# A transformer block on one core: four part buffers, weights loaded between the stores, merged score loads

## What is computed

```python
# x: (2, 2048, 256); 16 query heads, 4 key/value heads, head width 16
h = layernorm(x)
q, k, v = h @ Wq + bq, h @ Wk + bk, h @ Wv + bv
scores = einsum('bghnd,bhsd->bghns', q, k)           # g: 4 query heads share a key head
attn = softmax(scores / 4, axis=-1)
x = x + einsum('bghns,bhsd->bghnd', attn, v) @ Wo + bo
x = x + ffn(layernorm(x))                            # three cycles of a coupling net (cn_*, gc_*)
x = x + attn_b(layernorm(x))                         # Wg1 @ Wg2 makes its sigmoid gate
x = x + ffn(layernorm(x))
```

## Time and profile before

| | |
|---|---|
| median of 3 runs | 2151.23 us |
| the profiled execution, its own time | 2154.36 us |
| its span | 2152.4 us |
| TensorE's mean granted clock | 0.961 of full |
| busy: PE, PEld, DVE, ACT, POOL | 93%, 38%, 84%, 70%, 7% |

### The profile page before, as it was taken

How to read it: one execution, slowest core, us unless ns; L and a number is a source line. 1 busy time by engine, 2 the same in 40 slices (tenths; PEclk the granted TensorE clock), 3 DMA queues, 4 the chain that set the end, 5 groups by cost and what they waited for, 6 DMA issues and landing times.

```text
span 2152.4 us, 47834 instructions
## 1 busy us (share of the span) xinstructions
PE 2008.2 (93%) x13990; PEld 821.5 (38%) x13990; DVE 1814.5 (84%) x3396; ACT 1496.7 (70%) x2955; POOL 159.8 (7%) x290
## 2 busy tenths in 40 slices
PE   6699999999999999999999999989985899998984
PEld 4323333333333333333333333344432566665431
DVE  6789999999999999999999999934557677776456
ACT  4438888888888888888888888844558544446656
POOL 1340000000000000000000000010004101002001
PEclk9769999999999999999999999999997999999996
DMA  6421121121122122122122122131000000000002
GB/s 165 136 67 43 44 72 52 44 71 53 43 71 53 43 71 54 42 71 55 42 69 56 42 70 56 34 126 46 1 1 1 1 0 1 1 0 1 1 1 79
DMA packets 110229, 101.30 MB, mean 47 GB/s; under 512 B 52240, under 2 KB 91424, under 8 KB 110096
## 3 DMA queue, kind: packets, MB, share of 16 engines
q1 hardware_dynamic: 110096, 99.92, 17.2%
HBM read 78.79 MB, written 20.77 MB: 46 GB/s over the span
## 4 chain that ended last, share of the span: by engine, by line
PE 82%; DVE 6%; ACT 4%; issue 3%; SPq 3%; DMA 1%; ACTq 0%; POOL 0%; DVEq 0%; POOLq 0%
PE ps L697 22%; PE ps L672 15%; PE ps L720 10%; PE ps L726 10%; PE ps L840 6%; PE ps L847 3%; PE ps L900 3%; PE ps L909 2%; PE ps L929 2%; PE ps L948 2%; ACT YT L1088 1%; PE ps L686 1%; PE ps L979 1%; SPq L423 1%; DVE mx L1395 1%
## 5 line engine op out<-in xcount | busy, mean ns | idle before, releaser
L1395 DVE TENSOR_REDUCE mx<-ps 128x1 f32<-128x512 f32 x2048 | 1279.7, 683 | 20.2 <-PE ps L672 15.4
L1088 ACT ACTIVATE YT<-ps 128x512 f32<-128x512 f32 x2048 | 1058.1, 606 | 253.4 <-PE ps L726 253.3
L697 PE MATMUL ps<-YT,work 128*32 128x512 f32 x4096 | 546.1, 605 | 0.0
L672 PE MATMUL ps<-work 64*128 64x512 bf16 x2048 | 460.8, 389 | 17.7 <-DVE mx L1395 14.2
L720 PE MATMUL ps<-work 64*128 64x512 bf16 x2048 | 401.7, 378 | 1.7
L726 PE MATMUL ps<-work 34*128 34x512 bf16 x2048 | 398.3, 378 | 0.0
L672 PEld LDWEIGHTS ps<-work 64*128 64x128 bf16 x2048 | 144.6, 93 | 622.0 <-DVE mx L1395 548.3
L720 PEld LDWEIGHTS ps<-work 64*128 64x128 bf16 x2048 | 162.1, 94 | 106.0 <-ACT YT L1088 31.7
L847 PE MATMUL ps<-work,c_s 128*128 128x512 f32 x192 | 101.5, 655 | 30.9 <-ACT work L1139 30.9
L697 PEld LDWEIGHTS ps<-YT,work 128*32 128x32 f32 x4096 | 80.7, 108 | 122.8 <-issue 86.9
L726 PEld LDWEIGHTS ps<-work 34*128 34x128 bf16 x2048 | 101.0, 94 | 49.0 <-issue 1.3
(11 more groups left out here) (176 smaller groups left out, 1781.2 us busy)
## 6 DMA issues: line engine op xcount, KB each, us to landing
work<-k_scr SPq DMA_DIRECT2D x640, 64.0 KB, 2.1
work<-q_scr SPq DMA_DIRECT2D x640, 32.0 KB, 1.8
o_scr<-o_sb SPq DMA_DIRECT2D x32, 256.0 KB, 2.2
X<-in_L_attn_a_x_dram SPq DMA_DIRECT2D x8, 512.0 KB, 7.4
work<-negt SPq DMA_DIRECT2D x256, 1.0 KB
work<-o_scr SPq DMA_DIRECT2D x16, 256.0 KB
work<-inv_scr SPq DMA_DIRECT2D x16, 256.0 KB
out_dram<-X SPq DMA_DIRECT2D x8, 512.0 KB, 2.9
```

Source lines behind the costliest of these rows:

```text
L672: mm(ps[:, bank_of[x], :], qa[rows, p, jp, qt * P:(qt + 1) * P], ka[rows, p, kc_ * CH:(kc_ + 1) * CH], start=True, stop=True).then_inc(a_m ...
L697: m = mm(ps[32 * j:32 * j + 32, 7, :], vst[:, p, t, :], prob(GROUP * t + j), start=t == 0, stop=t == KTILES - 1)
L1088: fn(prob(u), ps[:, S_BANK + u % S_RING, :], ACT.Exp, scale=HD ** -0.5).then_inc(exp_ok, 1)
L1395: dve.tensor_reduce(mx[:, p, at_:at_ + 1], ps[:, bank_of[x], :], AX_X, ALU.max).then_inc(a_max, 1)
```

## The change

- **Part buffers:** both batches take all four in turn, chunk c the buffer c mod 4. Waits for a free buffer are for the chunk four before. `part_a` now holds chunks 4 and 5 too, so SP's first score loads and GpSimd's fills of kc and vst wait for the stores of chunks 2 to 5.
- **Weights:** six of the 36 later weights after the stores of each of the chunks 0 to 5.
- **Score loads:** `load_queries` issues 4 DMAs in place of 8 (32 rows by 2 pieces of 1 KB) and `load_keys` 4 in place of 8; the source of a key load is the same 16 rows read twice, with the repetition as its outermost dimension (stride 0, count 2), and 32 partitions as its destination. Both first score loads stand after chunk 5, the first query loads after chunk 1.
- **Negated maxima of step 0:** ahead of the last part's store of chunk 7 instead of after all stores.
- **Gate:** `gate_turn` and `gate_product` stand among the 16 maxima ahead, at x = 2 and x = 8. ScalarE's wait for the last stores goes.
- **Constants:** VectorE's ten operations stand after its last maxima.

```diff
-LOADED_MAX = 16 * 16
-LOADED = 16 * (16 + 8)
+LOADED_MAX = 16 * 8
+LOADED = 16 * (8 + 8)
...
         def part(c, pt):
-            return (part_a if c < CPG else part_b)[:, c % 2, pt]
+            return (part_a, part_b)[c // 2 % 2][:, c % 2, pt]
...
         def buffer_of(c):
-            return c // CPG * 2 + c % 2
+            return c % CPG
...
             if c >= 0:
-                eng.wait_ge(p_st[pt][buffer_of(c)], STORED * (c % CPG // 2 + 1))
-                eng.wait_ge(k_st[pt][buffer_of(c)], 16 * (c % CPG // 2 + 1))
+                eng.wait_ge(p_st[pt][buffer_of(c)], STORED * (c // CPG + 1))
+                eng.wait_ge(k_st[pt][buffer_of(c)], 16 * (c // CPG + 1))
...
-            for dst, src in weights:
-                sp.dma_start(dst, src).then_inc(w_ld, 16)
+            def load_weights(part):
+                for dst, src in weights[part::FREE]:
+                    sp.dma_start(dst, src).then_inc(w_ld, 16)
...
                         row = g * HALF + r * FINE
-                        for jp in range(JP):
-                            sp.dma_start(q_dst[row:row + FINE, p, jp],
-                                         q_scr[s, 2 * jp + g, 0:2].rearrange("r d n -> (r d) n")).then_inc(done[p], 16)
+                        sp.dma_start(q_dst[row:row + FINE, p],
+                                     q_scr[s, g:GROUP:2, 0:2].rearrange("j r d n -> (r d) j n")).then_inc(done[p], 16)
...
                         row = g * HALF + r * FINE
-                        for part_row in (row, row + HD):
-                            sp.dma_start(k_dst[part_row:part_row + HD, p], k_scr[kv_of(s), r]).then_inc(done[p], 16)
+                        src = k_scr[kv_of(s), r].rearrange("(a d) n -> a d n", a=1).broadcast_to((2, HD, SEQ))
+                        sp.dma_start(k_dst[row:row + FINE, p], src).then_inc(done[p], 16)
...
                 if c == CPG - 1:
                     for pt in range(2):
-                        for p in range(2):
-                            sp.wait_ge(k_st[pt][p], 16 * CPG // 2)
+                        for c4 in range(CPG):
+                            sp.wait_ge(k_st[pt][c4], 16)
                     load_keys(ka, 0, 0, qa_ld)
+                if c == NCH - 1:
+                    sp.wait_ge(nm_t, 1)
+                    load_negated(0)
                 store(c, 2, p_low)
-                if c == 0:
+                if c < FREE:
+                    load_weights(c)
+                if c == 1:
                     stored(sp, 0, 0)
                     stored(sp, 1, 0)
                     for s in (0, 1):
                         load_queries(qa, s, s, qa_ld)
                 if c == CPG:
                     load_keys(ka, 1, 1, qa_ld)
-                    stored(sp, 2, CPG - 2)
-                    stored(sp, 2, CPG - 1)
-                    load_scores(0, 0)
-                if c == NCH - 2:
-                    load_scores(1, 1)
+                if c == CPG + 1:
+                    for pt in range(3):
+                        for c4 in range(2, CPG + 2):
+                            stored(sp, pt, c4)
+                    for s in (0, 1):
+                        load_scores(s, s)
...
-            sp.wait_ge(nm_t, 1)
-            load_negated(0)
             refill_max(0, 0)
...
             for x in range(AHEAD):
+                if x == 2:
+                    pe.wait_ge(w_ld, 16 * len(weights))
+                    gate_turn()
+                if x == 8:
+                    gate_product()
                 max_mm(0, 1, x)
-            pe.wait_ge(w_ld, 16 * len(weights))
-            gate_turn()
-            gate_product()
...
                     if c not in (CPG, CPG + 1):
                         wait(act, p_low, c - 1)
-                        stored(act, 0, c - 2)
+                    stored(act, 0, c - CPG)
...
-                if c not in (CPG, CPG + 1):
-                    stored(act, 1, c - 2)
+                stored(act, 1, c - CPG)
...
-            for pt in range(3):
-                for c in (NCH - 2, NCH - 1):
-                    stored(act, pt, c)
...
-                if c not in (CPG, CPG + 1):
-                    stored(dve, 2, c - 2)
+                stored(dve, 2, c - CPG)
...
             negated_turn(STEPS - 1)
+            constants()
...
-                stored(pool, 2, c - 2)
+                stored(pool, 2, c - CPG)
...
             for pt in range(3):
-                for c in (CPG - 2, CPG - 1):
+                for c in range(2, CPG + 2):
                     stored(pool, pt, c)
-            pool.wait_ge(p_low, CPG)
+            pool.wait_ge(p_low, CPG + 2)
             pool.memset(kc[FINE:FINE_M], 1.0).then_inc(kb_ones, 1)
```

More of the change, by code:

```diff
@@ L1354, in _, with constants @@
                 low(c)
[L1356 to L1361, removed]
-            dve.tensor_copy(e3_s[:], last_c[0:64, 1:2].broadcast_to((64, P))).then_inc(cols, 2)
-            dve.tensor_scalar(half_b[:, 0:1], bias[:, D4:D4 + 1], 0.5, None, ALU.mult)
-            dve.tensor_scalar(half_b[:, 1:2], bias[:, F3:F3 + 1], 0.5, None, ALU.mult).then_inc(c_dve, 1)
-            dve.memset(coup[:, 2:3], 0.1)
-            dve.tensor_scalar(coup[:, 1:2], bias[:, AR:AR + 1], 0.3, None, ALU.mult)
-            dve.tensor_scalar(coup[:, 3:4], bias[:, AR:AR + 1], 0.7, None, ALU.mult).then_inc(c_dve, 1)
+            def constants():
+                dve.wait_ge(w_ld, 16 * len(weights))
+                dve.tensor_scalar(ct_s[:, 0, :], c1_s[:, 1, :], bias[:, SG:SG + 1], -1.0, ALU.mult, ALU.mult).then_inc(c_tw, 1)
+                dve.tensor_scalar(ct_s[:, 1, :], c1_s[:, 0, :], bias[:, SG:SG + 1], None, ALU.mult).then_inc(c_tw, 1)
+                dve.tensor_copy(w4_s[0:64, 0:1], last_c[0:64, 0:1])
+                dve.tensor_copy(w4_s[64:P, 1:2], last_c[64:P, 0:1])
+                dve.tensor_copy(c4_s[:], last_c[:, 0:1].broadcast_to((P, P))).then_inc(cols, 1)
+                dve.tensor_copy(e3_s[:], last_c[0:64, 1:2].broadcast_to((64, P))).then_inc(cols, 2)
+                dve.tensor_scalar(half_b[:, 0:1], bias[:, D4:D4 + 1], 0.5, None, ALU.mult)
+                dve.tensor_scalar(half_b[:, 1:2], bias[:, F3:F3 + 1], 0.5, None, ALU.mult).then_inc(c_dve, 1)
+                dve.memset(coup[:, 2:3], 0.1)
+                dve.tensor_scalar(coup[:, 1:2], bias[:, AR:AR + 1], 0.3, None, ALU.mult)
+                dve.tensor_scalar(coup[:, 3:4], bias[:, AR:AR + 1], 0.7, None, ALU.mult).then_inc(c_dve, 1)
             def row_maxima(s, p):
```

## The result

The changed kernel takes 2161.21 us (median of 5 runs, 2159.77 to 2162.49) against 2151.23 us (5 runs, 2150.05 to 2154.16): 1.0041 times as long, 95% interval 1.0028 to 1.0053, so slower by about 0.4%. The prediction was 2161 us. That the number is right is luck: its account is wrong in two of its terms, and their errors happen to cancel. In what follows one execution of one kernel, k_split_scores (2503.47 us at a granted clock of 0.739, the others 0.960 to 0.963), is left out of its ratio as slow.

What follows compares the result with a forecast made beforehand. It took the lead-in before the first L726 as what could move, with TensorE-bound steps unchanged. Merged keys on two engines outweighed a 23.5 us gain: 2151.23 + 9.9 = 2161 us, range 2126 to 2176.

Steps and rivals of the forecast that it cites:

- Buffers: Lead-in: two ScalarE stops of about 6.3 us go, low(5) ends at 67.5 instead of 79.8, gaining 12.3 us.
- Constants: VectorE's ten operations at the end: about 2.1 us, at most 3.0, under 4.7 us of cover, so no cost.
- Gate: Lead-in, among the sixteen maxima: no stall counted, at most the 2 us of the small matmuls.
- The merged key load: Key loads: two DMA engines instead of sixteen, 14.3 us a load_keys, with all queued behind the keys waiting.
- rival A: Key loads spread over all engines or onto others than the stores: 23.5 or 20 us less; chance 0.20.
- the ledger of engine 0: Lead-in: 96.3 us of gapless queue from 58.8 moves the first L726 from 145.89 to 155.8, +9.9 us.
- SP would have issued the keys for step 0 by 61: Lead-in, SP's queue: by issue time, step 0's keys are all issued by 61 us.
- the lower bound: DMA packet price: 0.175 us for 4 KB, from the store of o_sb, against the 0.223 us taken.
- rival B: Lead-in: two engines with packets at the lower bound, L726 at 143, total 2144 to 2152 us; chance 0.20.
- The steps. Cost nothing: Steps: two engines busy 32.9 of 40.1 us, so no cost, with a margin of 3.5 us a load_keys.
- my account of the steps is wrong: Stated test: the conclusion if the first L726 comes as said, at 155, and the time does not.
- In issue time all fits: Lead-in, by SP's issue time alone: ready for negated maxima at 109, first L726 at 122.4, 23.5 us less.

Runs made afterwards that it cites:

- k_split_scores: The changed kernel with only the scores' key loads split into eight DMAs again: 2154.79 us, 1.0013 of the kernel before.
- k_merge_only: The kernel before with the merged key loads alone: 2158.25 us, 1.0034 of the kernel before.
- k_split: The changed kernel with each key load as two DMAs of 16 rows again: 2144.57 us, 0.9968 of the kernel before.
- after_pad: The changed kernel with six long-satisfied wait instructions more ahead of ScalarE's loop: 2153.82 us, 1.0005 of the kernel before.
- k_split_late: The changed kernel with split key loads, six satisfied ScalarE waits, gate weights after chunk 0, other 34 after the first refill: 2133.47 us, 0.9917 of before.

## Why the prediction was right and wrong

**What held.** *Buffers:* `low(5)` ends at 66.9 (said: 67.5), and ScalarE has no stops of 6 us. *Constants:* cost nothing at the end, 1.34 us (estimate 2.1) under a cover of 4.7, of which 3.4 are left; and k_merge_only bears out that it was GpSimd's fills that made them slow. *Gate:* no stall to be seen; its worth when it decides is 4.3 us, not the 2 us of the matmuls, because each pair has a copy of ScalarE's behind it. *The merged key load:* two engines (share 0.12), keys 13.7 us from issue to the matmul that waited for them (5.5 in k_split), and what stands behind them held up in its turn, all as said; the other side, rival A, is refuted by k_merge_only and k_split.

**What failed first: the ledger of engine 0, +9.9 us.** It measured +0.7. The ledger was to run from 58.8 to 155.1. Its head was late: SP issued the keys at 64.04, since it had the stores ahead issued only at 61.9 and then waited for those of the keys to land, 1.9 us ("SP would have issued the keys for step 0 by 61" counted issue time alone). So the first maxima came at 77.7 instead of 74.1 and the turn at 126.36 instead of 121.3. The keys' first packet moved at 65.5, and its length from there to the landing of the negated loads (146.3) was 81 us in place of 96.3: 6.7 late and 15.5 shorter. The term that was mis-sized is the packet. I took 0.223 us for 4 KB from a window where all sixteen engines had keys in turn (16 rows outermost, a share of 0.45), and called 0.175 the lower bound. Two engines alone take 0.167, below that bound; over the 64 packets of each engine in the first `load_keys` it is 0.19 (65.5 to 77.5, with weights and stores between them). The trace has a time for each packet: ahead of the first L732 the 640 packets of 4 KB take 0.182 us on average, in before 0.241. At 16 DMAs of 16 packets 0.182 makes 10 us of the 15.5. The other 5 are not in the store packets, which took 0.054 us and not 0.051; no run separates them. That the two engines had work without a gap holds nearly, as far as the share can tell (at least 0.11 in every half microsecond from 65.5 to 145 but for 108 to 109). In the lead-in it is rival B, "L726 at 143", that came closest, with a chance of 0.20. One bound of the range is slightly off: 28.8 us of store packets at 0.044 instead of 0.051 are 4 us less, not 5.

**What failed next: "The steps. Cost nothing".** For the keys this is right: no step waits for them, and the steps are alike with the keys merged and split. But ScalarE's twelve removed waits stand in the diff, and the prediction has no term for them. They moved the head of ScalarE's loop by six instructions and cost 7.7 us over 13 jumps, and 7.7 by the ratios of after and after_pad. The trace of before had the sign of it, every second step 40.6 to 41.0; I read one early step, 40.1 (181.55 to 221.63), and took it for all.

So +9.9 was written for +0.7 in the lead-in, of which nothing is left at the second turn (181.32 in both), and 0 for +7.7 in the steps. The forecast named its own test, that if "the time does not" come with the first L726, "my account of the steps is wrong". The reverse happened: the time came and the first L726 did not, and the account was wrong all the same. Between the spans there are 7.0 us and between the medians 10.0; the 3 us between are the profiled execution of before, which was 3.1 above its median, as the prediction had noted. Nothing in the sum foresaw the steps, so its agreement with the median is luck.

**"In issue time all fits", first L726 at 122.4.** SP was to be ready for the negated loads at 109. In k_split, where single issues are mostly undisturbed, it reaches them at 125.38 and the first L732 comes at 131.81. It took up the first keys some 5 us later than counted (63.77; 2 us of issue that end at 61 start at 59), and four `load_keys` in eight cost it 3.6 us each where the count, with four DMAs at 0.5, has 2.0: 6.5 us more. The rest is spread over the other issues. So SP's issue time was counted too short, and k_split, with its 16 more issues, is not quite the case that was counted. With the weights out of the way, k_split_late gives 122.26: close to the figure, but by a kernel that is not the change.

**What stays open:** why 441 instructions ahead wait longest and 483 fetch nothing; what makes an issue of SP's take 2 to 3 us when two engines' queues are deep; how the rest of the ledger's 15.5 us is shared out; and what the four part buffers and the merged query loads are worth each by itself, since no run takes them back.

## What to carry to other kernels

Here halving the number of key DMAs lost time, since their shape left two engines at work: read the count of the outermost dimension and the DMA share before counting issues. A loop's cost per pass can hang on where its head lies in an engine's program; when instructions leave or enter ahead of a long loop, look at the instruction queues of the page and at one turn per step over all steps, and pad the head if passes differ. A prediction that comes out right in its total should still be held to each of its terms.

## What was not expected of the hardware

- Satisfied waits, executed once ahead of ScalarE's loop of 294 instructions, changed the kernel's time by 28 us between the best and the worst count tried (70: 2126.01, 28: 2153.66); with 70 the instruction queue q14 moved 33 packets in place of 97.
- Issuing half as many key DMAs, each twice as large, took 2.71 us in place of 3.59 (k_split) for a `load_keys`, 0.68 us each in place of 0.45: three quarters of the issue time, not half of it.
- While two DMA engines were loaded with merged keys, SP's issue of some unrelated stores and weights rose from 0.55 to between 2 and 3 us each (2.94 at 90.40 in after); in k_split the longest store issue of that stretch is 1.3 us.
- Packets of 4 KB took 0.182 us on average ahead of the first L732 with merged keys (0.183 in k_merge_only), and 0.237 to 0.241 with split ones (k_split, before).
- VectorE's ten constants took 7.7 us beside GpSimd's fills (before) and 1.4 us in the same place without them (k_merge_only).
